# One run of weighted values for each group of four heads, earlier inverse sums and a rarer double copy in an attention block

## The reference

```python
q, k, v = (proj(Wq, bq), proj(Wk, bk), proj(Wv, bv))      # [batch, head, 1024, 32]
scores = jnp.einsum('bhqd,bhkd->bhqk', q, k) * SCALE
scores = scores * (adj_matrix + bond_matrix)[:, None, :, :]   # both are adj
attn = jax.nn.softmax(scores, axis=-1)
ctx = jnp.einsum('bhqk,bhkd->bhqd', attn, v)
return jnp.einsum('bse,fe->bsf', ctx, Wo) + bo
```

## Time and profile before

| | us |
|---|---|
| median of three runs | 3097.78 (3092.64 to 3099.89) |
| the profiled execution: its span, the only time that the page gives | 3095.1 |
| TensorE busy | 3003.2 (97%) |
| VectorE busy | 1888.6 (61%) |
| ScalarE busy | 1492.7 (48%) |
| GpSimd busy | 690.9 (22%) |
| mean granted TensorE clock | 0.994 of full speed |

### The profile page before, as it was taken

One profiled execution on the slowest core, in us unless ns is written; L12 is line 12 of the kernel. 1 busy time (PEld: TensorE's weight loads), 2 busy tenths in 40 slices (PEclk: granted clock), 3 DMA queues, 4 the chain that ended last, 5 costly groups with the idle time before them and its releaser, 6 DMA issues.

```text
span 3095.1 us, 63393 instructions
## 1 busy us (share of the span) xinstructions
PE 3003.2 (97%) x22896; PEld 2340.7 (76%) x22896; DVE 1888.6 (61%) x4154; ACT 1492.7 (48%) x2745; POOL 690.9 (22%) x1241
## 2 busy tenths in 40 slices
PE   7999999999999999999999999999999999999999
PEld 6677786777877777778777787777867788677886
DVE  2688426884268742787437874378643786438863
ACT  1684217843178331783327832277322773238732
POOL 0243002430024300242002420034200342003410
PEclk9999999999999999999999999999999999999999
DMA  4302213022130221302313013121122212221200
GB/s 168 90 2 89 76 69 90 2 89 81 64 90 2 89 106 45 83 2 89 130 31 73 22 70 130 44 61 48 58 115 56 48 56 73 91 68 36 77 11 14
DMA packets 98905, 204.35 MB, mean 66 GB/s; under 512 B 11024, under 2 KB 42128, under 8 KB 98576
## 3 DMA queue, kind: packets, MB, share of 16 engines
q1 hardware_dynamic: 98576, 199.96, 20.7%
HBM read 136.75 MB, written 8.65 MB: 47 GB/s over the span
## 4 chain that ended last, share of the span: by engine, by line
PE 80%; DVE 6%; SPq 5%; issue 4%; ACT 3%; DMA 1%; POOL 0%; DVEq 0%; ACTq 0%; POOLq 0%
PE ps L1077 37%; PE ps L1224 14%; PE ps L1300 10%; PE ps L1252 8%; PE ps L1202 6%; SPq L446 4%; PE ps L1372 4%; DVE stats L608 1%; DVE h L845 1%; PE ps L1114 1%; ACT Z L1002 1%; DVE junk L829 1%; DMA qS<-qlo 1%; DVE hT L663 1%; ACT h2T L1033 1%
## 5 line engine op out<-in xcount | busy, mean ns | idle before, releaser
L787 DVE CUSTOM_DVE_ANT_0 Z<-ps,adjN 128x1024 f32<-128x1024 f32 x512 | 622.2, 1216 | 101.5 <-PE ps L1202 101.5
L1002 ACT ACTIVATE Z<-Z,nm 128x1024 f32<-128x1024 f32 x512 | 588.3, 1149 | 30.7 <-POOL nm L545 26.9
L1224 PE MATMUL ps<-ident,Z 128*128 128x128 f32 x4096 | 550.4, 278 | 13.7 <-DVE PTa L742 6.5
L1224 PEld LDWEIGHTS ps<-ident,Z 128*128 128x128 f32 x4096 | 455.0, 141 | 125.8 <-issue 75.7
L1202 PE MATMUL ps<-kS,qS 128*128 128x512 f32 x1024 | 370.8, 444 | 27.6 <-DMA qS<-qlo 27.6
L557 POOL TENSOR_SCALAR H<-adjN 128x128 fp32r<-128x128 f32 (+1 forms) x456 | 316.8, 695 | 0.0
L534 POOL TENSOR_SCALAR ve<-mv 128x4 f32<-128x4 f32 x80 | 15.7, 197 | 1331.4 <-DVE mv L613 1330.8
L545 POOL TENSOR_TENSOR nm<-nm,minus 128x1 f32<-128x1 f32 x512 | 97.1, 190 | 750.0 <-DVE nm L787 750.0
L1077 PE MATMUL ps<-mh,adjT 128*128 128x256 f32 x1024 | 223.6, 379 | 0.0
L1077 PE MATMUL ps<-v,P 128*128 128x257 f32 x1024 | 223.6, 379 | 0.0
L1077 PE MATMUL ps<-hT,t3T 128*128 128x512 f32 x512 | 221.0, 592 | 0.0
(11 more groups left out here) (170 smaller groups left out, 5712.7 us busy)
## 6 DMA issues: line engine op xcount, KB each, us to landing
adjT<-adjT_in SPq DMA_DIRECT2D x8, 4096.0 KB, 13.1
adjN<-adj_in SPq DMA_DIRECT2D x8, 4096.0 KB, 17.7
adjT<-adjT_in SPq DMA_DIRECT2D x8, 2048.0 KB, 9.1
qS<-qhi SPq DMA_DIRECT2D x112, 128.0 KB, 2.5
qS<-qlo SPq DMA_DIRECT2D x112, 128.0 KB, 2.5
kS<-khi SPq DMA_DIRECT2D x96, 128.0 KB, 2.4
kS<-klo SPq DMA_DIRECT2D x96, 128.0 KB, 2.5
adjT<-adjT_in SPq DMA_DIRECT2D x8, 1536.0 KB, 12.0
```

The costliest lines, as they stand in the source:

```text
L787: dve.tensor_tensor_reduce(Z[:, u % ZS], ps[:, 2 * (u % 2):2 * (u % 2) + 2].rearrange("p a n -> p (a n)"), adjN[:, u // HEADS], SCORE_SCAL ...
L1002: act.activation(Z[:, u % ZS], Z[:, u % ZS], ACT.Exp, bias=nm[:, u:u + 1], accum_out=sm[:, u:u + 1]).then_inc(exps.sem, 1)
L1224: mm = pe.transpose(ps[:, turn_bank((u, s)), rows(a)], Z[:, u % ZS, rows(NT // 2 * s + a)], ident[:])
```

## The change

The weighted values of a group are no longer two runs of 32 products at lags 6 and 7, but one run of 64 at lag 7. The spreading of the inverse sums goes from lag 5 to 4 and its copy on ScalarE from 6 to 7. VectorE makes the inverse sums before its copy of that iteration and not after. ScalarE copies both halves of the unit at place 5 of each row tile (8 in a batch), where it was every sixth unit (10 in a batch); the counts that the semaphores are waited on with follow. One condition is written with another name and has the same value.

```diff
--- before.py
+++ after.py
@@ -43,7 +43,7 @@
     HPG = P // HD
     GROUPS = HEADS // HPG
     UNITS = NT * HEADS
-    BOTH = 6
+    BOTH = 5
     PTS = 8
     PTA = 4
     ZS = 3
@@ -244,8 +244,8 @@
         nms = signal("nms", UNITS)
         exps = signal("exps", UNITS)
         T_ps = signal("T_ps", 2 * UNITS)
-        PT_act = signal("PT_act", UNITS + UNITS // BOTH)
-        PT_dve = signal("PT_dve", UNITS - UNITS // BOTH)
+        PT_act = signal("PT_act", UNITS + NT)
+        PT_dve = signal("PT_dve", UNITS - NT)
         pv_ps = signal("pv_ps", NT * GROUPS)
         R_ps = signal("R_ps", NT)
         invs = signal("invs", NT)
@@ -309,8 +309,8 @@
-        INVERT, SPREAD, COPY, WEIGH, NORMALISE, PROJECT, ADD = 4, 5, 6, 6, 9, 10, 11
-        PARTS = (NT // 2, NT // 2)
+        INVERT, SPREAD, COPY, WEIGH, NORMALISE, PROJECT, ADD = 4, 4, 7, 7, 9, 10, 11
+        PARTS = (NT,)
         BESIDE = {1: ("v", 1), 2: ("q", KQ_FIRST + 1), 4: ("v", 2), 5: ("v", 3)}
@@ -349,15 +349,15 @@
         def evacuates_both(u):
-            return u % BOTH == BOTH - 1
+            return u % HEADS == BOTH
         def by_act(u):
-            return u + 1 + (u + 1) // BOTH
+            return u + 1 + (u + HEADS - BOTH) // HEADS
         def by_dve(u):
-            return u + 1 - (u + 1) // BOTH
+            return u + 1 - (u + HEADS - BOTH) // HEADS
@@ -777,7 +777,7 @@
                 for u in range(STEPS):
                     if u == UNITS + 3:
                         split_h(0, 0, 1, 2)
-                    if u == UNITS - HPG + PROJECT:
+                    if u == UNITS - HPG + NORMALISE + 1:
                         split_h(0, 3, 4)
                     if u < UNITS:
                         dve.wait_ge(*S_ps(b, u + 1))
@@ -800,10 +800,10 @@
                         statistics(b, 2, t, x[:, t])
                     if (t := tile_due(u, ADD + 2)) is not None:
                         aggregate(b, 2, t)
+                    if (t := tile_due(u, INVERT)) is not None:
+                        inverse_sums(t)
                     if 2 <= u < UNITS + 2:
                         evacuate(u - 2)
-                    if (t := tile_due(u, INVERT)) is not None:
-                        inverse_sums(t)
                 split_h(1, *range(TPH, NT + 1))
```

## The result

The changed kernel takes 3079.91 us (median of four runs, 3078.4 to 3083.0), the kernel before 3096.88 (3092.6 to 3099.9). The ratio is 0.9946, with a 95% interval from 0.9935 to 0.9958: faster by 17 us, more than the 6 us (0.2%) under which the prediction counted a difference as none. The forecast was 3075, its range 3048 to 3096.

What follows compares the result with a forecast made beforehand. TensorE, busy 97%, was taken to bound the kernel. Six periods of 0.43 us less, plus 0.2 at the ends, give 2.8 us a batch, 22 for eight: 3097.8 to about 3075, range 3048 to 3096.

Steps and rivals of the forecast that it cites:

- The period: Time of one row tile between projections: 15.80 without waits plus 0.51 and 0.33, 16.64 us against 17.07 before.
- The wait of the run for the spread sums: A run in the kernel before waits 0.25 us for ScalarE's copy of the spread sums; forecast to go.
- The two added waits: TensorE's new waits before the transposes of unit 2 (0.68, net 0.51) and unit 6 (0.50, net 0.33).
- The loop that was added up from the earlier trace: Unit 2, scores through VectorE, GpSimd and ScalarE to transposes: 3.93 us against 3.25 of TensorE work.
- here the new place of ScalarE's double copy acts: Unit 6: transposes wait for the first copy of unit 5, queued behind unit 6's exponential; 5.14 against 4.64 us.
- The sign that was named, a wait of 0.5: Wait of about 0.5 us before unit 6's transposes, named as showing the forecast right.
- Units 1 and 5: Units two after a run unit, called safe by little: 2.54 us of chain against TensorE's own 2.51.
- The loss of up to 0.3 in unit 1: Net loss before unit 1's transposes if making the inverse sums before VectorE's copy fails to remove the delay.
- Both rivals that made the kernel slower or equal: Gain eaten by waits in units 5 and 1 (3094, chance 0.13); slower by clock (3154) or both waits (3114), 0.11.
- The term "+0.2": Net gain at a batch's incomplete first and last tiles: +0.2 us, bounds -0.5 and +1.0.
- a few tenths won in the first tile: Gain assumed in a batch's first row tile, a few tenths of a us, part of the edge sum.
- 0.58 of entries: Saving per row tile from merging half runs: two prices of entering and leaving a run, 0.29 us each.

Runs made afterwards that it cites:

- the added transposes: Changed kernel plus four unused transposes per row tile, seven times a batch: 3078.75 us with them in unit 0, 3105.03 in unit 7.
- the long run alone: Kernel before with only the weighted values in one run of 64 at lag 7, all else as before: 3156.96 us, ratio 1.0198.
- the mixed kernel: Changed kernel with each row tile's second group in two half runs again, first in one long run, spread-sums copy at lag 6: 3067.74 us.
- the sums alone: Kernel before with only the spreading at lag 4 and the inverse sums before VectorE's copy: 3079.99 us, ratio 0.9949.

## Why the prediction was right

**The period, right for the right sum.** 16.64 forecast, 16.59 measured. The run unit is 3.38 (forecast 3.39), the wait before unit 2 is 0.67 (0.68), and the way from the transposes behind the run to unit 6 is 5.11 (5.14). The wait of the run for the spread sums is gone. The two added waits cost what the forecast gave them: unit 2 takes 1.80 (907.79 to 909.59, 0.46 more than 1.34; forecast 0.51), and units 5 and 6 take 1.52 and 1.55, together 0.39 more than twice 1.34 (forecast 0.33). The middle of a batch won 0.473 a tile instead of 0.43.

**Unit 2.** The loop that was added up from the earlier trace rows is the one that acts, as the added transposes show. Its links in the changed kernel, VectorE and then ScalarE:

```profile
905.86 1.23 DVE L787 CUSTOM_DVE_ANT_0 Z<-ps,adjN 128x1024 f32<-128x1024 f32 x1
```

```profile
907.40 1.15 ACT L1002 ACTIVATE Z<-Z,nm 128x1024 f32<-128x1024 f32 x1 [0.42 <-POOL nm L545]
```

From the scores (904.90) 0.96 to the masked product, 1.54 to the exponential, 1.36 to the transposes: 3.86 where the rows of before gave 3.93.

**Unit 6: right time, wrong culprit.** The prediction put the wait on the new place of the double copy. ScalarE in this unit:

```profile
915.47 1.15 ACT L1002 ACTIVATE Z<-Z,nm 128x1024 f32<-128x1024 f32 x1 [0.42 <-POOL nm L545]
...
916.62 1.06 ACT L992 ACTIVATE PTb<-ps 128x512 f32<-128x512 f32 x2
```

The first of the two copies starts at 916.62 and the transposes that it releases follow 0.63 later, at 917.25. This first copy is there with or without the double one. What the double copy does is to spare the second half a wait of 0.40 for VectorE. The step that failed is "here the new place of ScalarE's double copy acts". The chain that was added up there is right, but it belongs to the projection's turn in the rotation of banks, and the place was given no gain of its own: VectorE's part was judged by its busy time, not by the order in its queue. With the double copy back at every sixth unit this wait stays and the kernel is 20 us slower. The sign that was named, a wait of 0.5, shows as 0.14 before the projection and 0.27 before the transposes, as the forecast said that an earlier short wait would be absorbed.

**Units 1 and 5, the clock.** The prediction called these units safe, though by its own sum (2.54 against 2.51) they are late by 0.03. In unit 5 the transposes come 0.39 behind the scores (914.30 to 914.69) instead of 0.35; in unit 1 nothing shows. The rows do not fix distances to hundredths, as the prediction said itself, so it is in part luck that neither cost more. The loss of up to 0.3 in unit 1, should the inverse sums not be earlier, does not exist: with them late the period is 16.60. The clock stayed at 1.00 in the tiles. Both rivals that made the kernel slower or equal fell.

**The ends, wrong.** The term "+0.2" was -0.7 a batch: 0.17 at the front, 0.33 at the end, 0.19 at the start within its scatter. That is 7 us of sum, partly offset by the tiles (0.04 x 48 = 2 us), and the forecast's 22 us became 17. The prediction took "a few tenths won in the first tile" without walking it. The first tile has no projection in unit 6, but the last of the projections for v that BESIDE puts beside the units stands in unit 5. TensorE's load for the transposes of unit 6, then ScalarE:

```profile
884.11 0.86 PEld L1224 LDWEIGHTS ps<-ident,Z 128*128 128x128 f32 x8 [0.98 <-issue]
```

```profile
882.26 0.60 ACT L983 ACTIVATE v<-ps 128x512 f32<-128x512 f32 x1 [1.53 <-PE ps L1077]
882.76 1.14 ACT L1002 ACTIVATE Z<-Z,nm 128x1024 f32<-128x1024 f32 x1
```

ScalarE waits 1.53 for that projection, copies it, and has the exponential of unit 6 queued behind the copy, although GpSimd had the maximum ready at 876.60. The transposes come 1.35 behind the exponential, after a wait of 0.98. It is the pattern of the long run alone again: a copy that waits for TensorE stands in ScalarE's queue ahead of an exponential. In the kernel before a half run in unit 6 filled this time, and the mixed kernel with that half run put back won 0.48.

At the end the prediction expected to lose 0.2 because unit 62 has no half run any more. The loss came, but that reason does not hold: with half runs again the stretch is 9.56, as long as with the long run (9.57). It is 9.24 with the double copy at place 5 alone and 9.43 with the sums alone. Without the small parts the long run does lengthen the end, to 10.05. Beside them it adds nothing, and the loss is theirs; the last section says what of it is traced.

**What the prediction did not say, though its numbers held it.** 0.58 of entries against 0.51 + 0.33 of waits is a long run that costs 0.26 a tile. Measured against half runs with the same small parts it costs nothing in the tiles and 5 us at the front. The gain of 17 us is that of the small parts. On half runs the sums' new order gives 16 us, the double copy's place 10, and both together 26. On the long run the parts are worth other amounts: the new lags of the sums 59 us, which only pay back what the long run had lost, then the place 20, and the earlier inverse sums nothing. The prediction walked the whole and never asked what each part would do by itself.

## What to carry to other kernels

When one engine is busy 97% and every unit makes a round through three others, work of that engine is not only a cost: between issuing and fetching it is the cover. Before two pieces are merged, add up the round (here 3.9 us) and the work that stays between its ends (3.25) for each unit, ends and first tiles too, and look in every queue of the round for a copy that waits for a late producer ahead of the instruction that counts; merge where there is enough, keep apart where there isn't. A part that looks like the accessory of a change, such as two lags, may be what makes it bearable, so test each alone.

## What the runs showed of the hardware

At the end of a batch one of VectorE's instructions that normalise x for the next layer (L770) took 0.73 instead of 0.41 us in the changed kernel, while GpSimd's last piece of the incidence ran. GpSimd and VectorE, timeline:

```profile
1003.11 3.66 POOL L557 TENSOR_SCALAR H<-adjN 128x1024 fp32r<-128x1024 f32 x1
...
1005.12 0.74 DVE L770 TENSOR_SCALAR h<-x,rstd,nmr 128x256 f32<-128x256 f32 x2
1005.83 0.43 DVE L774 SCALAR_TENSOR_TENSOR hl<-h,hh 128x256 fp32r<-128x256 f32 x1
1006.17 0.73 DVE L770 TENSOR_SCALAR h<-x,rstd,nmr 128x256 f32<-128x256 f32 x1
...
1007.16 0.41 DVE L755 TENSOR_TENSOR ctxn<-ps,Rs 128x256 f32<-128x256 f32 x1
```

The same place in the kernel before:

```profile
1010.77 3.64 POOL L557 TENSOR_SCALAR H<-adjN 128x1024 fp32r<-128x1024 f32 x1
...
1012.91 0.41 DVE L770 TENSOR_SCALAR h<-x,rstd,nmr 128x256 f32<-128x256 f32 x1
...
1013.73 0.42 DVE L755 TENSOR_TENSOR ctxn<-ps,Rs 128x256 f32<-128x256 f32 x1
1014.07 0.49 DVE L770 TENSOR_SCALAR h<-x,rstd,nmr 128x256 f32<-128x256 f32 x1
```

In the changed kernel GpSimd's instruction ends at 1006.77 and VectorE's slow one at 1006.90, 0.13 later. In the kernel before the ends are 1014.41 and 1014.56, and the instruction that ran into the end of GpSimd's took 0.49. In the kernel with half runs the same instruction took 1.00 us, and in that with the double copy at every sixth unit up to 1.27. The Trainium skill ("SBUF — State Buffer", section "SBUF: two separate sides") says that the two engines share a pair of ports which one instruction holds for its whole length while the other waits; on VectorE's side this holds for an instruction in a two-port mode, or for one with two inputs in SBUF while GpSimd's reads SBUF. The ends of the slow instructions agree. But two of the same kind at 1005.12 took an ordinary 0.74 together within GpSimd's 3.66 us, and so did the next one, with two inputs in SBUF (1005.83, 0.43), so the whole rule is not what this trace shows. The profile gives spans on GpSimd only roughly, and why the third alone was held stays open.

Counted from the seventh projection (998.81 and 1005.72), the third instruction starts 0.17 later than in the kernel before, and the normalisation of the context that follows it (L755) 0.34 later. So about half of the 0.33 us that the end of a batch lost arises here, and the other half before it was not traced.
